# Graph attention over a sparse adjacency: the last two tiles routed, filled and indexed in two parts, their row matrix made on ScalarE, and another order at the end

## The reference

```python
h = x @ W
e = (h @ a[:128, 0])[:, None] + (h @ a[128:, 0])[None, :]
e = jnp.where(e > 0, e, 0.2 * e)
e = jnp.where(adj > 0, e, -9e15)
attention = softmax(e, axis=1)
y = x + elu(attention @ h)
out = (y - mean(y)) / sqrt(var(y) + 1e-5)      # over the 128 columns
```

## Time and profile before

| | us |
|---|---|
| median of 3 runs | 714.63 |
| lowest, highest | 712.79, 715.48 |
| the profiled execution, own time | 716.63 |
| its span, first to last instruction | 714.8 |
| mean granted TensorE clock in it | 0.874 |

### The profile page before, as it was taken

One profiled execution on the slowest core, in us unless ns is written; L12 is line 12 of the kernel. 1 busy time (PEld: TensorE's weight loads), 2 busy tenths in 40 slices (PEclk: granted clock), 3 DMA queues, 4 the chain that ended last, 5 costly groups with the idle time before them and its releaser, 6 DMA issues.

```text
span 714.8 us, 11813 instructions
## 1 busy us (share of the span) xinstructions
PE 558.3 (78%) x3025; PEld 352.9 (49%) x3074; DVE 479.6 (67%) x2059; ACT 521.6 (73%) x416; POOL 447.1 (63%) x676
## 2 busy tenths in 40 slices
PE   0867887776979787777788778887787988887985
PEld 0323455453546554544555555554455555545564
DVE  2375577776585867677666667677666577675774
ACT  0847778787877887878788777878787788787601
POOL 2015367767575776677666766767667577677771
PEclk9979999988887989999999988899999688888976
DMA  9999999999999999999999999999999999999362
GB/s 352 328 416 429 426 424 426 426 423 425 425 427 429 426 426 428 427 427 426 427 425 427 431 425 426 428 427 427 428 426 428 431 425 426 426 427 423 128 182 73
DMA packets 34598, 285.57 MB, mean 399 GB/s; under 512 B 5528, under 2 KB 13872, under 8 KB 18064
## 3 DMA queue, kind: packets, MB, share of 16 engines
q1 hardware_dynamic: 29024, 276.83, 92.7%
q0 software_dynamic: 5120, 8.42, 3.3%
q10 hardware_dynamic: 432, 0.07, 0.1%
HBM read 283.18 MB, written 4.19 MB: 402 GB/s over the span
## 4 chain that ended last, share of the span: by engine, by line
DMA 64%; PE 16%; ACT 11%; issue 4%; DVE 2%; POOL 1%; SPq 1%; ACTq 0%; POOLq 0%; DVEq 0%
DMA adj_sb<-in_adj 62%; ACT adj_squared L603 10%; PE fold L718 8%; DMA a_sb<-in_L_gnn_a 2%; PE x_att_ps L771 1%; PE misc L748 1%; PE fold L714 1%; PE fold L830 1%; PE small L733 1%; PE small L757 1%; POOL edge_row L375 1%; SPq L413 1%; PE x_att_ps L774 0%; PE h_ps L798 0%; PE fold L785 0%
## 5 line engine op out<-in xcount | busy, mean ns | idle before, releaser
L603 ACT ACTIVATE adj_squared<-adj_sb 128x4096 bf16<-128x4096 int32 x128 | 462.5, 3614 | 105.6 <-DMA adj_sb<-in_adj 99.7
L718 PE MATMUL fold<-adj_sb,bit_ident 128*128 128x512 bf16 x993 | 302.9, 449 | 10.2 <-DMA adj_sb<-in_adj 4.8
L528 POOL DMA_INDIRECT nb<-in_x,index x160 | 165.9, 1037 | 90.3 <-issue 59.8
L718 PEld LDWEIGHTS fold<-adj_sb,bit_ident 128*128 128x128 bf16 x1024 | 110.8, 108 | 154.2 <-issue 68.1
L953 DVE MAX8 top_map<-fold 128x8 f32<-128x512 f32 x128 | 89.3, 699 | 70.7 <-PE fold L718 57.0
L714 PE MATMUL fold<-col_no,ident_bf 128*128 128x512 bf16 x112 | 47.8, 426 | 104.9 <-DMA adj_sb<-in_adj 90.9
L375 POOL TENSOR_SCALAR edge_row<-row_iota,edge_in 128x128 f32<-128x128 int32 x186 | 128.9, 707 | 0.0
L393 POOL TENSOR_TENSOR spread<-edge_row,edge_w 128x384 f32<-128x384 f32 x60 | 55.0, 935 | 74.6 <-DVE edge_w L1079 74.6
L508 POOL TENSOR_SCALAR empty_diag<-ident,counts 128x128 f32<-128x128 f32 x64 | 39.5, 623 | 64.3 <-DVE counts L989 33.5
L714 PEld LDWEIGHTS fold<-col_no,ident_bf 128*128 128x128 bf16 x128 | 16.4, 128 | 125.0 <-issue 86.8
L771 PEld LDWEIGHTS x_att_ps<-spread,nb 128*128 128x128 f32 x372 | 57.5, 221 | 8.0 <-issue 4.1
(11 more groups left out here) (139 smaller groups left out, 631.2 us busy)
## 6 DMA issues: line engine op xcount, KB each, us to landing
adj_sb<-in_adj SPq DMA_DIRECT2D x127, 2048.0 KB, 14.8
out<-x_sb SPq DMA_DIRECT2D x2, 1536.0 KB
nb<-in_x,index POOLq DMA_INDIRECT x160, 2.4
adj_sb<-in_adj SPq DMA_DIRECT2D x2, 1024.0 KB, 17.0
out<-x_sb SPq DMA_DIRECT2D x4, 128.0 KB
out<-x_sb SPq DMA_DIRECT2D x1, 384.0 KB
out<-x_sb SPq DMA_DIRECT2D x2, 64.0 KB
W_sb<-in_L_gnn_W ACTq DMA_DIRECT2D x1, 64.0 KB, 7.8
```

Of the source, the lines that this page charges most:

```text
L528: nc.gpsimd.indirect_dma_start(out=nb_of(j, g)[:, c, :], out_offset=None, in_=x[:, :], in_offset=bass.IndirectOffsetOnAxis(ap=index[:, g, ...
L603: nc.scalar.activation(adj_squared[:, h % 2, :], adj_sb[:, h % LOAD_SLOTS, :], ACT.Square, accum_out=half_sum[:, h:h + 1]).then_inc(square ...
L718: last = nc.tensor.matmul(fold[:, h % LOAD_SLOTS, :], bit_ident[:, b, :], adj_low[:, h % LOAD_SLOTS, b * FOLD:(b + 1) * FOLD, 0], start=Fa ...
```

## The change

Five things, all in the part written out by hand behind the loop.

1. `route(*final)` becomes `route_tiles()`: the comparison and the matrix of tile 0, then those of tile 1, each with a semaphore of its own (`tile_routed`). GpSimd's `tally(*final)` waits for the second.
2. `fill_edges(*final)` and `indices(*final)` become `fill_parts()` and two calls of `part_indices(p)`. Part 0 is chunks 0 and 1, part 1 is chunks 2 to 4 and uses bank 2 of `fold`. `gather(*final)` waits for part 0 ahead of chunk 0 and for part 1 ahead of chunk 2.
3. The final group's `edge_row` is made on ScalarE: six Squares of (edge's row number minus column counter) into a new tile `apart`, then one Relu of 1 minus that over all 768 columns. DVE's six comparisons and its wait for `spread_ready` go.
4. On ScalarE `copy_sums(*back2)` stands ahead of `exp_weights(*back1)`, not behind it; the new function stands ahead of both.
5. Spare products: 4, 5 and none at the last three places become 8, 8 and 2.

```diff
+        PARTS = [(0, CHUNKS // PAIR), (CHUNKS // PAIR, CHUNKS)]
+        part_edges = [edge_in_ps, fold[:, 2, 0:CHUNKS * SENT].rearrange("p (c k) -> p c k", k=SENT)]
...
                 def gather(j, g):
-                    hold(pool, indexed, count(j, g), pool_spare)
+                    if not is_final(j, g):
+                        hold(pool, indexed, count(j, g), pool_spare)
...
                     for c in range(CHUNKS):
+                        for p, (lo, hi) in enumerate(PARTS):
+                            if is_final(j, g) and c == lo:
+                                pool.wait_ge(part_indexed[p], 1)
...
                 exp_elu(*back3)
+
+                def last_edges_to_rows():
+
+                    j, g = final
+                    act.wait_ge(part_read[0], 1)
+                    act.wait_ge(part_read[1], 1)
+                    act.wait_ge(spread_ready, count(*back2))
+                    act.wait_ge(t_sent, count(*back2))
+                    for t in range(PAIR):
+                        for k, c in enumerate(SPANS[t]):
+                            last = nc.scalar.activation(apart[:, t, k, :], row_iota[:, t * P:(t + 1) * P], ACT.Square,
+                                                        bias=edge_in[:, c, ROW_COL:ROW_COL + 1], scale=-1.0)
+                    last.then_inc(rows_apart, 1)
+                    act.wait_ge(rows_apart, 1)
+                    nc.scalar.activation(edge_row[:, g, :, :, :].rearrange("p t k c -> p (t k c)"),
+                                         apart[:].rearrange("p t k c -> p (t k c)"), ACT.Relu,
+                                         bias=ones[:, 0:1], scale=-1.0).then_inc(edge_row_made, 1)
+
+                last_edges_to_rows()
+                copy_sums(*back2)
                 exp_weights(*back1)
-                copy_sums(*back2)
                 exp_elu(*back2)
...
+                def fill_parts():
+
+                    g = final[1]
+                    for p, (first_c, end_c) in enumerate(PARTS):
+                        pe.wait_ge(tile_routed[p], 1)
+                        for t in range(PAIR):
+                            for c, lo, hi, e in pieces(t):
+                                if first_c <= c < end_c:
+                                    last = nc.tensor.matmul(part_edges[p][lo:hi, c, :], row_edge[:, g, t, e:e + hi - lo],
+                                                            sent[:, t, :], start=True, stop=True)
+                        last.then_inc(part_filled[p], 1)
...
                 keep_warm(7)
-                fill_edges(*final)
+                fill_parts()
                 sum_neighbours(*back2)
                 send_scores(*back1)
                 times_W(*back2)
-                keep_warm(4)
+                keep_warm(8)
                 send_shares(*back1)
-                keep_warm(5)
+                keep_warm(8)
                 send_scores(*final)
+                keep_warm(2)
                 sum_neighbours(*back1)
...
+                def route_tiles():
...
+                    for t in range(PAIR):
+                        v.after(nc.vector.tensor_scalar(below_end[:, t, :], edge_no[:, t, :], ends[:, t:t + 1], None,
+                                                        ALU.is_lt))
+                        nc.vector.scalar_tensor_tensor(
+                            row_edge[:, g, t, :], edge_no[:, t, :], sent[:, t, START_COL:START_COL + 1],
+                            below_end[:, t, :], ALU.is_ge, ALU.mult).then_inc(tile_routed[t], 1)
+
+                def part_indices(p):
+                    g = final[1]
+                    lo, hi = PARTS[p]
+                    part = [P, hi - lo, SLOTS]
+                    dve.wait_ge(part_filled[p], 1)
+                    nc.vector.tensor_copy(edge_in[:, lo:hi, :], part_edges[p][:, lo:hi, :]).then_inc(part_read[p], 1)
+                    dve.wait_ge(part_read[p], 1)
...
+                    nc.vector.tensor_scalar(index[:, g, lo:hi], edge_code[:, lo:hi], -1.0, float(COL_0),
+                                            ALU.mult, ALU.add).then_inc(part_indexed[p], 1)
...
-                route(*final)
-                indices(*final)
+                route_tiles()
+                dve.wait_ge(edge_row_made, count(*back1))
+                for p in range(2):
+                    part_indices(p)
                 neighbour_scores(*back1)
                 finish(*back3)
                 scores(*back1)
-                dve.wait_ge(spread_ready, count(*back2))
-                edges_to_rows(nc.vector, *final)
                 weights(*back1)
```

More of the change, by code:

```diff
@@ L171, in graph_attention @@
         index = sb("index", [P, GROUPS, CHUNKS], u32)
+        apart = sb("apart", [P, PAIR, SPAN, P], fp32)
         edge_row = sb("edge_row", [P, GROUPS, PAIR, SPAN, P], fp32)
@@ L260, in graph_attention @@
         first_t = sem("first_t")
+        tile_routed = [sem(f"tile_routed{t}") for t in range(PAIR)]
+        part_filled = [sem(f"part_filled{p}") for p in range(2)]
+        part_read = [sem(f"part_read{p}") for p in range(2)]
+        part_indexed = [sem(f"part_indexed{p}") for p in range(2)]
+        rows_apart = sem("rows_apart")
         tile_summed = [sem(f"tile_summed{t}") for t in range(PAIR)]
@@ L518, in tally @@
                                           ).then_inc(sums_kept, 1)
-                    hold(pool, routed, count(j, g), pool_spare)
+                    if is_final(j, g):
+                        pool.wait_ge(tile_routed[PAIR - 1], 1)
+                    else:
+                        hold(pool, routed, count(j, g), pool_spare)
                     nc.gpsimd.tensor_copy(counts_all[:, :, tiles], counts[:]).then_inc(tallied, 1)
                 def gather(j, g):
-                    hold(pool, indexed, count(j, g), pool_spare)
+                    if not is_final(j, g):
+                        hold(pool, indexed, count(j, g), pool_spare)
                     if not first(j) and not is_final(j, g):
@@ L1026, in indices @@
                                             ALU.mult, ALU.add).then_inc(indexed, 1)
+                def route_tiles():
+                    j, g = final
+                    dve.wait_ge(starts_made, count(j, g))
+                    v.after(nc.vector.tensor_tensor(sent[:, :, START_COL], starts_ps, tile_edge[:], ALU.add))
+                    v.after(nc.vector.tensor_tensor(ends, sent[:, :, START_COL], found, ALU.add))
+                    for t in range(PAIR):
[11 more added lines that the diff above has]
+                    dve.wait_ge(part_read[p], 1)
+                    v.after(nc.vector.tensor_tensor(
+                        at_slot[:, g, lo:hi, :], edge_less_slot[:, lo:hi, :],
+                        edge_in[:, lo:hi, START_COL:START_COL + 1].to_broadcast(part), ALU.is_equal))
+                    v.after(nc.vector.tensor_tensor(own_code[:, lo:hi, :], edge_in[:, lo:hi, 0:SLOTS],
+                                                    at_slot[:, g, lo:hi, :], ALU.mult))
+                    v.after(nc.vector.reduce_sum(edge_code[:, lo:hi], own_code[:, lo:hi, :], AX.X))
+                    if p == 0:
+                        dve.wait_ge(gathered[g], final[0] * (16 * CHUNKS))
+                    nc.vector.tensor_scalar(index[:, g, lo:hi], edge_code[:, lo:hi], -1.0, float(COL_0),
+                                            ALU.mult, ALU.add).then_inc(part_indexed[p], 1)
                 def neighbour_scores(j, g):
```

## The result

The changed kernel takes 710.72 us (median of 20 runs, 709.33 to 712.06), the kernel before 715.38 us beside it (20 runs, 711.57 to 719.98). The ratio is 0.9929, 95% interval 0.9912 to 0.9945, which makes 5.1 us less; the medians themselves lie 4.7 us apart. The forecast was 709.7 us, 707.2 to 713.9. The profiled execution took 709.52 us with a span of 707.7, where the one of before took 716.63 and 714.8.

The account below looks back on a forecast made before the run. Bounds: the load of adj to about 665 us, then TensorE's queue, partly at half clock. With the clock high, finish_tile(0) comes 5.9 us earlier: profiled 716.63 to 710.7; middle with 708.7 gives 709.7 us, range 707.2 to 713.9.

Parts of the forecast that it names:

- The clock stays up: At the end, TensorE's idle time before the product with W shrinks from 1.8 to 0.2 us, keeping 2.4 GHz.
- forecast tail gain: Behind the load, finish_tile(0) starts 5.9 us earlier, and all behind it to the last store is unchanged.
- a cost and a risk: Nine more spare products on TensorE's queue: 3.8 us if the clock falls and stays low to 704.
- The sum along TensorE's queue: From the product with W at 685.5 to back1's last shares at 696.6, before 701.6: 5.0 us, clock high.
- The gathers: Last group on GpSimd: first gather at 682.0, last at 687.6, 1.1 us earlier (bounds 0 and 1.3).
- The row matrix on ScalarE: Last group: squares 2.4 us, Relu up to 1.0, ready at 685.1, off the path; 0.8 us back on VectorE.
- VectorE just in front of the last tiles: At the end, finish(*back1) ends at 700.6, later than TensorE's 700.45, and stands just before finish_tile(0).
- From the profiled execution to the median: Whole run: profiled execution goes to 710.7; median is 710.7 or 708.7, so the middle, 709.7, was taken.
- the sum's own forecast for the profiled execution: Whole profiled execution: from 716.63 to 710.7 us, with finish_tile(0) 5.9 us earlier.
- The slower one: TensorE's end: clock low to 704, nine more spare products cost 3.8 us, giving 718.5 us; chance 0.08.
- One drop and a return, the first rival: TensorE's end: clock drops once, returns in the first eight spare products, 1.4 us less gain, 711.1 us; chance 0.18.
- the other two: Before the product with W: slower ScalarE leaves the gap, 712.9 us, chance 0.10; Relu reloads tables, 713.9, chance 0.04.

Follow-up runs that it names:

- b_copy_spare: Kernel before with only the copy of back2's sums ahead of back1's exponential and spare products 8, 8, 2; 711.05 us, ratio 0.9936.
- a_late: Changed kernel with the copy of back2's sums behind the exponential of back1 again; 714.12 us, ratio 0.9967.
- a_few: Changed kernel with the old spare products (4, 5, none); 713.38 us, ratio 0.9980.
- a_dve_rows: Changed kernel with the six comparisons back on VectorE, between scores and weights of back1, none of it on ScalarE; 711.15 us, ratio 0.9920.
- a_whole: Changed kernel with the last two tiles routed, filled and indexed whole, as in the old code; 711.27 us, ratio 0.9928.
- b_spare: Kernel before with only the spare products of the change (8, 8, 2 for 4, 5, none); 714.58 us, ratio 0.9977.
- a_tally: Changed kernel with GpSimd's tally of the last group moved behind its gathers; 711.96 us, ratio 0.9937.
- after: The changed kernel itself, against the kernel before; 710.72 us, ratio 0.9929.
- b_copy: Kernel before with only ScalarE's order changed: copy of back2's sums ahead of the exponential of back1; 714.64 us, ratio 0.9984.
- a_again: The changed kernel itself, measured once more beside other variants on one chip; 711.04 us, ratio 0.9941.

## Why the prediction was right, and where it was not

*The clock stays up.* Right, and the heart of it. The last product is at 699.57 and no window of the tail up to 704 reads below 1.00. The forecast tail gain was 5.9 us, the measured one 6.2. b_copy_spare shows that the copy and the spare products together are sufficient for nearly all of it, a_late and a_few that each is necessary. The prediction priced them apart and treated the spare products as a cost and a risk; without them no gain is left that can be told from none (a_few). That step was misjudged, and here the right number owes something to luck: it said the clock would stay up because the pause shrinks, and a_few, with the pause gone, has the clock down, while a_dve_rows has it down once with TensorE's pauses as in the changed kernel. What triggers a fall no run here settles.

*The sum along TensorE's queue*, on the time axis of before's profile (0.91 us added): product with W 685.65 (forecast 685.5), shares of back1 688.0 to 689.3 (688.1 to 689.4), scores of the last group 691.05 (691.35), sums 693.2 (693.3), last shares ended 696.4 (696.6), `finish_tile(0)` 700.3 (700.6). Every point is within 0.3 us. Two errors offset each other in front of the product with W: the scores of back1, which were to stay where they were, began 0.5 us later (see the gathers), and the row matrix and the copy were 0.2 us earlier than forecast, so the product waited for the scores and not for the copy. And from here on the chain is VectorE's list, where the forecast added up TensorE's queue; the two run so close together (`first_t` was there at 690.00, the scores behind the second eight began at 690.14) that the sum came out.

*The gathers.* Mis-sized. The first began at 682.7 on that clock, 0.5 us earlier than before and not 1.1; the last at 687.95 (forecast 687.6). The forecast overlooked that GpSimd's spread would run beside the first part's small operations. The same step was to leave `neighbour_scores(*back1)` within 0.1 us of its old time; on before's axis it began at 682.79 and not at 682.26, 0.5 us late. Of the 0.5 us that the gathers did gain, a_whole, with the old routing and indexing, has 0.2 already. That they gained less than forecast cost nothing, since `finish(*back2)` on VectorE held the first of the last group's products until 688.81 (689.72 on before's axis) anyway.

*The row matrix on ScalarE.* Squares 0.29 us apart and not 0.40 (each takes 0.39, so they overlap), 1.86 us in all for 2.4; the Relu 0.94 for 1.0; no second table load. Off the path, as said. Its worth on VectorE was to be 0.8 us; a_dve_rows shows none that could be told from zero. The traces show where it went. Counted from the first spare product the shares of back1 are ready at 14.4 us in b_copy_spare, which has neither part, at 13.4 in a_whole, which has only the row matrix on ScalarE, and at 14.1 in the changed kernel. Of the 1.0 us between the first two, 0.2 lie ahead of both parts (the counts' products, L726 and its twins, come at 3.26 us in b_copy_spare and at 3.05 in the other two). So the row matrix gave its 0.8 us there, and the split took 0.7 back. So the two parts that make up most of the diff, the split and the row matrix, bring 0.4 us of tail at most (34.8 or 35.2 against b_copy_spare's 35.3).

*VectorE just in front of the last tiles.* Right: `finish(*back1)` ended at 699.41 and `finish_tile(0)` began at 699.37.

*From the profiled execution to the median.* The middle between 710.7 and 708.7 was a guess and happened to fit (710.7 was the better of the two). In the trace the 716.63 became 709.52: 6.2 us by the tail and 0.9 by the part in front of it. The runs gained 5.1 us by the ratio. So the sum's own forecast for the profiled execution, 710.7, was 1.2 us too high, and that the median of 20 runs reads 710.72 is in part luck. Whether the tail of before is shorter in other runs stays open, since before has one profile only.

*The rivals.* The slower one needed the clock low to 704 under more spare products; b_spare, the nearest case, has the clock back at the end of the first eight and comes out level with before. One drop and a return, the first rival, is what a_tally and a_dve_rows show in the changed kernel's near neighbours, but with the return only about 693, behind the second eight, and tails of 37.9 and 37.3 us: the margin is small. Of the other two, no gap was left in front of the product with W, and no second table load came.

## What to carry to other kernels

Where a queue of small products bounds a stage, look at the granted clock before looking at the work: two edits, ordering an old copy first and filling TensorE's waits with wide products, gave 0.64% together and alone nothing that could be told from zero, because either one alone left a place where the clock fell. Filler costs nothing up to the length of the wait it fills and most of its price behind that, and a wait that it just fills can no longer hide a delay in front of it. And before an operation on VectorE is moved earlier, see what GpSimd does at that moment.

## What the runs showed of the hardware

- The granted clock fell around 12 products with 10 columns and two pauses of 0.6 to 0.7 us (a_few), and stayed up across pauses of 0.98 and 0.78 us (after) and of 1.49 us (b_copy). Behind the same products and the same pauses it stayed up in one program (after) and fell inside 686 to 688 in another (a_dve_rows).
- Nine more spare products made a kernel faster: 711.05 us against 714.64 (b_copy_spare, b_copy).
- A single-input VectorE comparison of 128x320 took 2.20 us beside GpSimd's 1.63 us tensor_tensor, 0.39 us alone (a_tally); two-input operations of 128x20 took 0.65 and 0.76 us beside it (after), 0.18 alone (a_tally).
- Square with a bias operand, 128 columns: 0.39 us each, 0.29 us apart. Relu with one, 768 columns: 0.94 us.
- Up to 4 us of this kernel's spread lie ahead of the part that was changed: the first spare product came between 672.77 and 676.85 in the profiled executions, latest where the clock was low while the last halves were folded (a_again, a_gaps).
